# Moving one interleaved projection matmul behind the attention-value matmuls of the same step, in a causal attention and low-rank FFN layer on eight cores

## The reference

```
polymax(s) = (s*s + 1) / 1000      for s > 0
           = (1 - s/100) / 1000    for -100 <= s <= 0
           = 0                     below -100, and where the key is after the query
h = layernorm(x);  q, k, v = split(h @ W_attn)
x = x + (polymax(q k^T / 8, causal) @ v) @ W_proj
g = layernorm(x)
x = x + gelu(g @ U1 @ V1 + b1) @ U2 @ V2 + b2
```

## Time and profile before

| | us |
|---|---|
| median of 2 runs (2089.01 and 2095.27) | 2092.14 |
| profiled execution, device time | 2090.82 |
| its span (slowest core, core 7) | 2089.2 |
| shortest span of a core (core 2) | 2065.5 |
| attention half 0 on core 7 | 515 to 1174 |

### The profile page before, as it was taken

How to read it: one execution, slowest core, us unless ns; L and a number is a source line. 1 busy time by engine, 2 the same in 40 slices (tenths; PEclk the granted TensorE clock), 3 DMA queues, 4 the chain that set the end, 5 groups by cost and what they waited for, 6 DMA issues and landing times.

```text
span 2089.2 us, 22723 instructions; the slowest of 8 cores (2065.5 to 2089.2 us)
## 1 busy us (share of the span) xinstructions
PE 1322.7 (63%) x6880; PEld 460.7 (22%) x6880; DVE 1259.0 (60%) x2171; ACT 760.1 (36%) x1074; POOL 0.2 (0%) x4
## 2 busy tenths in 40 slices
PE   3423295577887787777778337666774551468886
PEld 0001042243222222222112013322221220023332
DVE  3657433234778898989889423588996233344422
ACT  1100000000556676767677300267775000033333
POOL 0000000000000000000000000000000000000000
PEclk8655597889556676777677679755666775579998
DMA  5435201200000000000000320000001443001111
GB/s 166 161 121 195 87 20 62 80 1 11 12 17 16 19 6 16 8 16 6 18 16 6 106 61 1 1 1 1 1 1 36 165 140 101 0 0 41 40 41 41
DMA packets 53334, 96.07 MB, mean 46 GB/s; under 512 B 2529, under 2 KB 24290, under 8 KB 53218
## 3 DMA queue, kind: packets, MB, share of 16 engines
q1 hardware_dynamic: 46498, 84.14, 12.3%
q10 hardware_dynamic: 6720, 10.49, 1.7%
HBM read 82.04 MB, written 12.58 MB: 45 GB/s over the span
## 4 chain that ended last, share of the span: by engine, by line
PE 48%; DVE 24%; issue 12%; DMA 11%; ACT 3%; SPq 1%; DVEq 1%; ACTq 0%
DVE poolD L765 11%; PE ps L799 8%; DMA poolD<-W_attn 6%; PE ps L731 5%; PE ps L847 5%; PE ps L1124 3%; PE ps L933 3%; PE ps L632 3%; PE ps L654 3%; PE ps L612 3%; PE ps L1030 3%; PE ps L1144 3%; DMA poolD<-W_proj 1%; DVE poolC L498 1%; DMA poolD<-x_t 1%
## 5 line engine op out<-in xcount | busy, mean ns | idle before, releaser
L752 ACT ACTIVATE poolD<-ps 128x1024 bf16<-128x1024 f32 (+3 forms) x640 | 559.7, 900 | 835.8 <-PE ps L731 729.5
L765 DVE SCALAR_TENSOR_TENSOR poolD<-poolD 128x1024 bf16<-128x1024 bf16 (+3 forms) x640 | 652.0, 1058 | 34.8 <-ACT poolD L757 12.6
L799 PE MATMUL ps<-poolD,poolA 128*64 128x512 bf16 (+3 forms) x1280 | 302.2, 460 | 170.3 <-DVE poolD L778 89.0
L731 PE MATMUL ps<-poolB,poolA 64*128 64x512 bf16 (+3 forms) x1280 | 278.8, 462 | 34.1 <-ACT poolD L757 16.7
L799 PEld LDWEIGHTS ps<-poolD,poolA 128*64 128x64 bf16 x1280 | 88.6, 118 | 364.7 <-issue 364.7
L847 PE MATMUL ps<-poolC,poolD 128*128 128x512 bf16 x256 | 132.1, 516 | 30.3 <-DVE poolD L712 30.3
L1136 ACT ACTIVATE poolC<-ps,sb_b1s 128x512 bf16<-128x512 f32 x128 | 87.9, 687 | 115.5 <-PE ps L1124 75.9
L757 ACT ACTIVATE poolD<-ps,consts 128x256 bf16<-128x256 f32 x256 | 123.7, 483 | 0.0
L731 PEld LDWEIGHTS ps<-poolB,poolA 64*128 64x128 bf16 x1280 | 64.7, 102 | 230.0 <-issue 228.8
L933 PE MATMUL ps<-poolD,poolC 128*128 128x512 bf16 x256 | 60.7, 392 | 54.1 <-DVE poolD L905 54.1
L807 PE MATMUL ps<-poolD,poolA 128*64 128x128 bf16 x512 | 83.8, 302 | 0.0
(11 more groups left out here) (101 smaller groups left out, 1146.4 us busy)
## 6 DMA issues: line engine op xcount, KB each, us to landing
poolD<-x_t SPq DMA_DIRECT2D x8, 2048.0 KB, 9.9
poolA<-x_t SPq DMA_DIRECT2D x8, 2048.0 KB, 9.8
poolD<-W_attn SPq DMA_DIRECT2D x12, 1024.0 KB, 4.9
poolD<-W_attn SPq DMA_DIRECT2D x16, 512.0 KB, 4.0
poolC<-x_own_t SPq DMA_DIRECT2D x8, 1024.0 KB, 5.1
y<-poolC SPq DMA_DIRECT2D x4, 2048.0 KB, 6.6
kf2scratch<-poolD SPq DMA_DIRECT2D x32, 128.0 KB, 1.7
poolA<-kf2scratch SPq DMA_DIRECT2D x4, 1024.0 KB, 12.9
```

What stands on the lines that cost most here:

```text
L731: e.matmul(o, l, r, skip_group_check=True, start=True, stop=True, tile_position=tp),
L752: e.activation(o, i, AF.Relu), inc="S")
L765: e.scalar_tensor_tensor(o, i, 0.01, i, ALU.add, ALU.mult),
L799: e.matmul(o, l, r, skip_group_check=True, start=st, stop=True, tile_position=tp),
```

## The change

In `emit_attention`, the call `emit_av(idx)` moves from behind the K matmul of its step to ahead of it:

```diff
                         emit_eg(idx, fences[idx])
                         if idx + 3 < nk:
                             fences[idx + 3] = emit_qk(idx + 3)
+                        emit_av(idx)
                         if half == 0 and idx < 8:
                             b.wait("tensor", "V", kcast[hc])
                             if idx == 0:
                                 b.wait("tensor", "V", av_free[idle_bk])
                             b.op("tensor", lambda e, o=bank(idle_bk),
...
                                  e.matmul(o, l, r, skip_group_check=True, start=st,
                                           stop=sp), inc="T")
-                        emit_av(idx)
```

## The result

| | before | with the change |
|---|---|---|
| median | 2090.98 us (22 runs) | 2099.74 us (23 runs) |
| ratio | | 1.0037, 95% interval 1.002 to 1.0054 |
| profiled execution, device time | 2090.82 us | 2096.39 us |
| slowest core of the profiled execution | core 7, 2089.2 us | core 3, 2094.8 us |
| mean span of the eight cores, over runs (30, from the rounds of the experiments, and 23) | 2081.6 us | 2088.6 us |

In some executions of any of these kernels the cores of one die show a lower granted clock and take longer; the ratios and the means over runs leave those out. The change makes the kernel slower by 0.37%, 7.7 us. The prediction said 16 us slower on the same basis (2107 against 2091). The sign is right, the size is twice what was measured.

The account below looks back on a forecast made before the run. No engine bounds the whole kernel; in half 0 PE bounds c = 0, and PE at half clock, then DVE, bounds c = 1 to 3. 4.3 + 12 = 16.3 us on 2090.8 gave 2107 us, range 2093 to 2118.

Parts of the forecast that it names:

- K(0) runs for nothing ahead of AV(0): All 32 blocks of half 0: K(0) fills PE's wait for G(0); moved behind AV(0), it makes QK(4) 0.54 us later.
- the new neighbours: Matmul pairs in the new order, AV then K and K then QK: K step priced unchanged, ends +5 to -16 us.
- The term of c = 0: Eight blocks of c = 0, PE without slack: each 0.54 us longer at half clock, 4.3 us in all.
- at which all eight run on core 7: Step in the c = 0 term: all eight blocks run at half clock on core 7, so each costs 0.54 us.
- my rival of the clock: c = 0: clock up more often, each block won over gives 1.8 us plus 0.2; four give 2099, eight 2091; chance 0.14.
- The term of c = 1 to 3: 24 blocks: late QK adds to DVE's wait, 20 x 0.54 + 4 x 0.39 = 12.4 us, taken as 12.
- My walk through one block: Block of c = 2: QK(6), relu(6) and G(6) each move later, adding 0.54 us to DVE's 0.42 us wait.
- Absorbed: Rival, c = 1 to 3: late QK costs DVE nothing, only 4.3 us remain, 2095 us; chance 0.10.
- AV earlier pays: Rival: earlier G buffer release returns DVE's 0.42 us in 20 blocks, -8 us, 2082 to 2083; chance 0.06, shared with cheap neighbours.
- The clock rises later: Rival, c = 1 to 3: longer PE idle before AV(0) prolongs half clock, up to 54 us, 2161; chance 0.07, 0.05 past 2%.

Follow-up runs that it names:

- no_k0: Kernel before with K(0) left out in every block: c = 1 to 3 took 543.3 us, c = 0 108.6 us.
- k0_front: Changed kernel with K(0) put back ahead of AV(0), so only K(1) to K(7) moved: c = 1 to 3 543.7 us, ratio 1.0033 to before.
- k0_behind: Kernel before with only K(0) moved behind AV(0): c = 1 to 3 550.9 us, ratio 1.0015 to before.
- two_k0: k0_behind with K(0) issued twice behind AV(0): c = 1 to 3 559.0 us on cores 2 to 7, c = 0 108.4 us.
- spread: Kernel before with K in every second step for c = 1 to 3, K(0) and K(1) ahead of AV(0) for c = 0: ratio 0.9887, median 2070.61 us.
- late_av0: Kernel before with the first mask product of step 0 done twice more in c = 0, delaying AV(0): c = 0 117.3 us, c = 1 to 3 543.5 us.

## Why the prediction was half right

**K(0) runs for nothing ahead of AV(0), and costs when it comes behind: right.** no_k0 (543.3), k0_front (543.7) and k0_behind (550.9 us) show it from three sides. PE idle 0.72 us, AV(1) in its old place, QK(4) later by 0.54 us, a step of 1.65 us, the new neighbours at the price taken: each as written. DVE's wait was not: 0.42 us at G(5) in the block shown, where I had written 0.9 us at G(6).

**The term of c = 0, 4.3 us: the step "at which all eight run on core 7" failed.** The price of one slow block, 0.54 us, was right. But I took the clock as given. In the new order it rises in 85 of 128 blocks instead of 45. With the lengths from G(0) to L856 in the two samples of each (11.36 us without a rise and 10.10 with one before; 11.94 and 10.48 with the change) the old share of rises would have made c = 0 longer by 8 x 0.51 = 4.1 us; with the new share it is 8 x 0.05 = 0.4 us. So the clock gave back 3.7 us. That is my rival of the clock with 2.5 blocks of eight won over, each worth 1.5 us where I had put 2.0. I had given it 0.14 and had thought that it excluded the forecast; both happened at once, in different blocks. The forecast had no term for the clock, although the block of core 3 in the earlier trace rows stood at full clock. Resting the term on core 7 was a mistake of its own: its c = 0, 115.3 us without a single rise, was the longest of eight cores whose mean was 110.4. In the second sample core 7 has the longest again, 115.1 us with one rise, so it may be more than chance that the slowest core was the one without the clock.

**The term of c = 1 to 3, 12 us: mis-sized, 8.6 us measured.** It was 0.54 us for each of 20 blocks and 0.39 for four; it is 0.36 on the mean. Sorted by when the clock rose after G(0), the mean us from G(0) to the copy of the K tile (L856 before) in c = 2 and 3, for blocks that began at half clock:

| rise after G(0), us | 4.5 to 5.5 | 5.5 to 6.5 | 6.5 to 7.5 | 7.5 to 8.2 |
|---|---|---|---|---|
| before (two samples) | 19.28 | 19.63 | 20.03 | 20.27 |
| change (two samples) | 19.73 | 19.96 | 20.41 | 20.66 |
| k0_behind | 19.77 | 19.92 | 20.44 | 20.63 |
| two_k0 (cores 2 to 7) | 20.14 | 20.26 | 20.70 | 20.94 |
| spread (two samples, 151 blocks of 256) | 19.08 | 19.04 | 19.07 | 19.31 |

At an equal rise, one K matmul behind AV(0) costs 0.29 to 0.49 us and the second 0.26 to 0.37. My walk through one block had QK(6) late by 0.54, at half clock, and left the rise at the same step. The explanation that fits: the rise comes at a time, not at a step. PE is one K matmul behind when it comes, and works that off at full clock, where a K matmul is 0.32 us. What DVE loses is what PE is behind at about the rise, so the price should lie between 0.32 and 0.54, near the lower. The timeline above has the case: the clock rises at 847.7, within K(2), and QK(6) is only 0.39 us long. That the price is PE's arrears at the time of the rise would explain that the change and k0_behind cost the same at an equal rise, and roughly the two doses, although some of the values lie below 0.32. It is argued, not shown: no run held the rise fixed.

The sum by the measured terms: 0.4 + 8.6 is 9 us by parts, 8.6 by the lengths of all blocks, against 7.0 us more in the mean span over the runs and 7.7 us by the ratio. Behind half 0 the kernel before takes 914 us and the change 912 on the mean of two samples; two samples of one kernel lie 2.5 and 3.1 apart there, so no effect can be read.

**The other rivals.** "Absorbed" is out: DVE's wait grew in c = 1 to 3. "AV earlier pays" is out: k0_front has AV earlier in steps 1 to 7 and c = 1 to 3 are as before. "The clock rises later" is out: the K matmuls average 486 ns, well below the 560 that I had named for it. The Trainium skill (TensorE: Matmul & The Clock Gate, section HAM oscillation), which I had set beside that rival, is not contradicted: the longer pause ended at half clock in all of c = 1 to 3 before as well, and in c = 0, where I had wrongly written that each block starts at half clock, the clock was up at AV(0) in 12 and 15 of 64 blocks before and in 15 and 16 with the change. The 0.54 us more of pause brought down no clock that can be counted; what changed was the rise.

**Still open.** What makes the clock rise more often in c = 0. The kernels fall into two groups. Those with a K matmul ahead of AV(0) saw 22 to 28 rises of 64 (before 23 and 22, k0_front 22, late_av0 25, spread 28 and 25), those without saw 36 to 54 (no_k0 36, k0_behind 40, the change 43 and 42, two_k0 54). So most of the added rises go with the empty place ahead of AV(0), and a matmul behind AV(0) adds to them at most a part, since no_k0 has none there. Nor is the count of rises the whole of the clock: in spread it was up at AV(0) already in 21 and 22 blocks, and its mean granted clock over c = 0 is 0.67 with few rises, where it is 0.63 and 0.62 before and 0.69 and 0.68 with the change. Most of these are single executions, and a rise in one block moves the start of the next. No run here shows the cause.

## What to carry to other kernels

In a stage where engines take turns at being the bound, ask of a filler not how long it is but which wait it fills: moving one matmul of eight out of a wait cost 7.2 us in 24 blocks, and moving the others cost these blocks nothing. Put filler where the engine waits, and thin it out where the engine is the bound; that was worth 24 us here, with the same instructions, a part of it possibly through the clock. Price a delay at the clock at which it is worked off, and don't take the clock of one core in one execution for the kernel's: count it over all cores.

## What the runs showed of the hardware

A stage that waits in turns can get shorter with a matmul more in each block, through the clock. In c = 0, where a block takes 13.50 us at half clock and 11.70 at full, a repeated K(0) behind AV(0) went with 54 of 64 blocks with a rise, where the kernel before had 23, and with eight blocks of 108.4 us instead of 110.4. It is not that more work brings the clock: without any K(0) there were 36 rises and 108.6 us. The granted clock was sensitive to the place of a single 0.54 us matmul in a block of 13 us: averaged over runs and cores it is 0.7292 before (30 runs), 0.7344 with the change (23), 0.7343 with K(0) alone moved (7), and 0.7260 with the others moved (8).

In the kernel before and in the change, the clock was at half at AV(0) in every block of c = 1 to 3 and rose once in each, 4.6 to 8.7 us after G(0) in c = 2 and 3.
